# Attention in a vision tower: K for the transport plan by way of DRAM, and a share of each head's result added on VectorE

## What is computed

```python
qn = q / (norm(q) + 1e-8)
C = 1 - einsum('bhnd,bhmd->bhnm', qn, qn);  C = where(eye, 1000, C)
log_K = -C / 0.1
for _ in range(10):                                  # Sinkhorn
    log_u = log_marg - logsumexp(log_K + log_v[..., None, :], axis=-1)
    log_v = log_marg - logsumexp(log_K + log_u[..., :, None], axis=-2)
z = exp(log_u[..., :, None] + log_K + log_v[..., None, :])
z = z / max(z);  z = where(eye, 1, z)
out = softmax(z * hd ** -0.5) @ v
```

## Time and profile before

| what | value |
|---|---|
| median of 3 runs (lowest to highest) | 4995.21 us (4989.33 to 4996.69) |
| the profiled execution's own time, its span | 4997.56 us, 4995.8 us |
| mean granted PE clock | 0.959 |
| attention, 1390 to 3900 us of the span: PE, DVE, ACT busy | 2487.76, 2006.51, 1598.71 of 2510 us |
| DMA over the whole span | 232.97 MB, mean 47 GB/s |

### The profile page before, as it was taken

How to read it: one execution, slowest core, us unless ns; L and a number is a source line. 1 busy time by engine, 2 the same in 40 slices (tenths; PEclk the granted TensorE clock), 3 DMA queues, 4 the chain that set the end, 5 groups by cost and what they waited for, 6 DMA issues and landing times. The chain is left out here.

```text
span 4995.8 us, 192120 instructions
## 1 busy us (share of the span) xinstructions
PE 4573.8 (92%) x84693; PEld 3640.3 (73%) x84710; DVE 3718.4 (74%) x8486; ACT 3097.0 (62%) x4620; POOL 313.9 (6%) x347
## 2 busy tenths in 40 slices
PE   5999999975899999999999999999999879599992
PEld 3777777732688888888888888888888745277771
DVE  8999999944478888887887887777777745355556
ACT  4777777723566666666666666666666326377776
POOL 0000000000000000000000000000000005523331
PEclk9999999987899999999999999999999979699996
DMA  1010000023001111111111122100000024322224
GB/s 64 28 40 28 27 27 27 17 93 81 25 17 32 29 37 29 33 25 23 42 43 36 37 42 52 27 23 16 16 16 15 6 89 158 126 65 72 68 69 162
DMA packets 190201, 232.97 MB, mean 47 GB/s; under 512 B 81024, under 2 KB 159104, under 8 KB 187328
## 3 DMA queue, kind: packets, MB, share of 16 engines
q1 hardware_dynamic: 175872, 189.76, 14.0%
q0 software_dynamic: 13632, 32.66, 1.8%
HBM read 144.09 MB, written 78.25 MB: 45 GB/s over the span
## 5 line engine op out<-in xcount | busy, mean ns | idle before, releaser
L699 PE MATMUL y_ps<-k_sb,x_sb 128*12 128x256 f16 x58368 | 1694.9, 274 | 33.5 <-DVE x_sb L956 24.3
L699 PEld LDWEIGHTS y_ps<-k_sb,x_sb 128*12 128x12 bf16 x58368 | 1427.8, 88 | 218.2 <-issue 37.6
L829 ACT ACTIVATE y_sb<-y_ps 128x256 f32<-128x256 f32 x912 | 348.4, 382 | 856.2 <-PE y_ps L699 856.2
L838 ACT ACTIVATE k_new<-cos,k_bias 128x512 f32<-128x512 f32 x768 | 520.9, 683 | 171.7 <-PE cos L726 171.7
L709 PEld LDWEIGHTS turned_x<-rows_in,y_sb 128*128 128x128 f32 x3648 | 478.3, 191 | 120.2 <-issue 72.7
L987 DVE CUSTOM_DVE_ANT_0 plan<-plan,u_rows,v_last 128x512 f32<-128x512 f32 x768 | 535.2, 744 | 4.1
L709 PE MATMUL turned_x<-rows_in,y_sb 128*128 128x16 f32 x3648 | 527.1, 258 | 9.9 <-ACT y_sb L829 9.2
L257 PE MATMUL acc<-w_hl,feat_h 128*128 128x384 f16 x2688 | 455.3, 327 | 87.5 <-ACT feat_h L242 87.5
L852 ACT ACTIVATE plan<-plan,p_bias,p_scale 128x1024 f32<-128x1024 f32 x384 | 464.1, 1237 | 9.7 <-DVE p_scale L998 9.7
L975 DVE TENSOR_TENSOR plan<-k_sb 128x1024 f32<-128x1024 f16 x384 | 459.3, 1217 | 0.0
L1002 DVE TENSOR_TENSOR k_sb<-k_new,k_sb 128x2048 f16<-128x2048 f32 x192 | 436.2, 2272 | 29.8 <-ACT k_sb L846 29.8
(11 more groups left out here) (261 smaller groups left out, 7223.1 us busy)
## 6 DMA issues: line engine op xcount, KB each, us to landing
x_in_sb<-expert_rows SPq DMA_DIRECT2D x39, 528.0 KB
xt<-in_x_dram SPq DMA_DIRECT2D x16, 1280.0 KB, 5.8
q_left<-q_parts SPq DMA_DIRECT2D x192, 64.0 KB, 3.9
q_right<-q_parts SPq DMA_DIRECT2D x192, 64.0 KB, 3.9
raw<-in_w_dram SPq DMA_DIRECT2D x24, 384.0 KB, 4.3
w<-w_halves SPq DMA_DIRECT2D x16, 576.0 KB, 7.1
w<-expert_results SPq DMA_DIRECT2D x24, 384.0 KB, 6.4
v_parts<-v_sb SPq DMA_DIRECT2D x16, 408.0 KB, 2.4
```

What stands on the lines that cost most here:

```text
L699: last = nc.tensor.matmul(y[a][32 * c:32 * c + XW, :, :], high[:, j, XW * h:XW * (h + 1)], k_sb[s][:, h, :, at:at + P], start=(h == 0 and ...
L829: nc.scalar.activation(y_sb[a][:, :, :], y[a][:, :, :], ACT.Copy).then_inc(rows_read[a], 1)
L838: nc.scalar.activation(k_new[h % 2][:, c, :], cos[:, c % 2, :], ACT.Exp, bias=k_bias[:, 0:1], scale=1.0 / (REG * Q_SCALE ** 2), accum_out= ...
```

## The change

1. `join` goes, on DVE. SP's `store_k` sends each head's float32 `k_new` (1 MB) to `k_all`, a ring of five groups in DRAM, once ACT has written it; `load_k` brings it back into `plan[h]`, which now has four buffers, about one phase before `times_u` wants it. The other new waits: `exponents` for the store from that `k_new` two heads back, `times_u` for the load, `load_k` for the `times_v` that read the buffer last and for the store. `high_parts` no longer waits for `joined`.
2. `turn_v` has only L767's matmul. `normalise` begins with a `scalar_tensor_tensor` that adds (1 - exp(-scale)) times v to the turned result, 128 x 68 values, from PSUM into `lifted`; the reciprocal and the product read `lifted`.
3. The load of v waits for `att_ready` in place of `pv_turned`, since DVE now reads v too. SP clears `project`'s semaphores as it enters `attend`; one constant (`lift`) goes.

```diff
@@ attend, SyncE
+            def store_k(G, h):
+                H = (G + 1) * GH + h
+                after(sp, k_exp, (H + 1) * TB)
+                sp.dma_start(k_all[(G + 1) % RING, h, :, :], k_new[h % 2][:, :, :].rearrange("p b n -> p (b n)")).then_inc(k_out[h % 2], 16)
+
+            def load_k(F, h):
+                after(sp, pv_ready, (F - 1) * GH + h + 1)
+                after(sp, k_out[h % 2], 16 * ((F * GH + h) // 2 + 1))
+                sp.dma_start(plan[h][:, :, :].rearrange("p b n -> p (b n)"), k_all[F % RING, h, :, :]).then_inc(k_in[h], 16)
...
                 if old:
-                    after(sp, pv_turned, (G - 3) * GH)
+                    after(sp, att_ready, (G - 3) * GH)
                     load_v(t - 1 if s == 0 else t, (s + 2) % 3)
+                if build:
+                    store_k(G, 0)
+                if fin:
+                    load_k(G - 2, 3)
                 if tail:
                     after(sp, att_ready, (G - 2) * GH)
                     store(t - 1, s)
-
+                for h in range(1, GH):
+                    if build:
+                        store_k(G, h)
+                    if old:
+                        load_k(G - 1, h - 1)
@@ TensorE
                 after(pe, pv_read, H + 1)
-                nc.tensor.matmul(trp, lift[:, :], v_sb[s][:, :, h, :], start=True, stop=False)
-                nc.tensor.matmul(trp_flat, pv_sb[:, :], to_chunks, start=False, stop=True).then_inc(pv_turned, 1)
+                nc.tensor.matmul(trp_flat, pv_sb[:, :], to_chunks, start=True, stop=True).then_inc(pv_turned, 1)
@@ ScalarE
                     if c == 0:
                         after(act, k_built, H - 1)
+                        after(act, k_out[h % 2], 16 * (H // 2))
...
-                if fin:
-                    after(act, joined, (G - 2) * GH + h + 1)
@@ VectorE
                 if chunks[0] == 0:
-                    after(dve, joined, H + 1)
+                    after(dve, k_in[h], 16 * (F + 1))
                     after(dve, u_rows_ready, H + 1)
...
                 after(dve, pv_turned, H + 1)
-                nc.vector.reciprocal(den[:, :, :], trp[:, :, HD:HD + 1]).then_inc(den_ready, 1)
-                after(dve, den_ready, H + 1)
+                nc.vector.scalar_tensor_tensor(lifted[:, :, :], v_sb[s][:, :, h, :], float(1.0 - np.exp(-ATT_SCALE)), trp,
+                                               ALU.mult, ALU.add).then_inc(den_ready, 1)
+                after(dve, den_ready, 2 * H + 1)
+                nc.vector.reciprocal(den[:, :, :], lifted[:, :, HD:HD + 1]).then_inc(den_ready, 1)
+                after(dve, den_ready, 2 * H + 2)
...
-                nc.vector.tensor_tensor(att_sb[s][:, :, h, :], trp[:, :, 0:HD], den[:, :, :].to_broadcast([P, TB, HD]),
+                nc.vector.tensor_tensor(att_sb[s][:, :, h, :], lifted[:, :, 0:HD], den[:, :, :].to_broadcast([P, TB, HD]),
...
                         if fin:
-                            join(G - 2, new, a, 0)
-                            join(G - 2, new, a, 1)
                             times_u(G - 2, new, a, (0, 1))
```

More of the change, by code:

```diff
@@ L479, in _ @@
             images(dve, nothing, split, read_low)
+    return counters
 GH = 4
@@ L492 @@
 LARGEST_FROM, MAX_PHASE, SPLIT_FROM = 3, 18, 20
+RING = 5
 K_SHIFT = float(15 * np.log(2))
@@ L501, in after, with attend @@
         eng.wait_ge(counter, START + count)
-def attend(nc, q_parts, v_parts, ident, pick_rows, att, w, w_halves, unscale):
+def attend(nc, q_parts, v_parts, k_all, ident, pick_rows, att, w, w_halves, unscale, over):
     with ExitStack() as ctx:
@@ L538, in attend @@
         k_new = two("k_new", [P, TB, TOKENS], F32)
-        plan = two("plan", [P, TB, TOKENS], F32)
+        plan = [sb(f"plan{h}", [P, TB, TOKENS], F32) for h in range(GH)]
         y_sb = two("y_sb3", [P, 2, P], F32)
@@ L571, in attend @@
         cos_ready, k_exp, k_high, k_built = sem("cos_ready"), sem("k_exp"), sem("k_high"), sem("k_built")
-        joined, u_rows_ready, plan_ready, head_max_ready = (
-            sem("joined"), sem("u_rows_ready"), sem("plan_ready"), sem("head_max_ready"))
+        u_rows_ready, plan_ready, head_max_ready = sem("u_rows_ready"), sem("plan_ready"), sem("head_max_ready")
+        k_out, k_in = [sem(f"k_out{a}") for a in range(2)], [sem(f"k_in{h}") for h in range(GH)]
         max_rows_ready, all_max_ready, scale_ready, p_ready = (
@@ L582, in attend @@
         block = ctx.enter_context(nc.Block())
[L583 removed]
+        CONSTS, ZEROS = 6, 7
         def phases(eng, phase):
@@ L670, in phase @@
                     store(t - 1, s)
+                for h in range(1, GH):
[3 more added lines that the diff above has]
+                        load_k(G - 1, h - 1)
+            for counter in over:
+                sp.sem_clear(counter)
             sp.wait_ge(zeroed, START + ZEROS)
@@ L759, in times_v @@
                         last = nc.tensor.matmul(pv[32 * c:32 * c + HD + 1, 0:P], v_sb[s][:, j, h, :],
-                                                plan[h % 2][:, j, c * P:(c + 1) * P], start=(j == 0), stop=(j == TB - 1))
+                                                plan[h][:, j, c * P:(c + 1) * P], start=(j == 0), stop=(j == TB - 1))
                 last.then_inc(pv_ready, 1)
@@ L850, in weights @@
                     after(act, scale_ready, F * GH + h + 1)
-                part = plan[h % 2][:, 2 * half:2 * half + 2, :]
+                part = plan[h][:, 2 * half:2 * half + 2, :]
                 nc.scalar.activation(part, part, ACT.Exp, bias=p_bias[:, 0:1], scale=p_scale[h % 2][:, 0:1]).then_inc(p_ready, 1)
@@ L895, in phase @@
                         exponents(G, new, a, (2, 3))
-                        high_parts(G, new, a, fin)
+                        high_parts(G, new, a)
                     if c == 2 and build:
@@ L907, in phase @@
                         if build:
-                            high_parts(G, new, b, fin)
+                            high_parts(G, new, b)
                         if fin:
@@ L968, in old_x @@
                     split(tr[1], s, x_steps[1], (G - 1) * (OLD - 1) + i, x_new[1])
[L970 to L978, removed]
             def times_u(F, s, h, chunks):
@@ L986, in times_u @@
                 for c in chunks:
-                    last = nc.vector.tensor_tensor_reduce(plan[h % 2][:, c, :], plan[h % 2][:, c, :], u_rows[:, :],
+                    last = nc.vector.tensor_tensor_reduce(plan[h][:, c, :], plan[h][:, c, :], u_rows[:, :],
                                                           v_last[s][:, c, h:h + 1], 0.0, ALU.mult, ALU.max, row_max[:, c:c + 1])
@@ L1070, in phase @@
                         times_u(G - 2, new, a, (2, 3))
-                        join(G - 2, new, b, 0)
                     if c == 2:
@@ L1074, in phase @@
                             low_parts(G, new, a)
-                        if fin:
-                            join(G - 2, new, b, 1)
                     if c == 3:
@@ L1973, in tower @@
         clear(nc, embed(nc, x, freqs, w_tok, h))
-        project(nc, h, wqv, ident, q_parts, v_parts)
+        over = project(nc, h, wqv, ident, q_parts, v_parts)
         unscale = ctx.enter_context(nc.sbuf_tensor("unscale4", [P, 2], F32))
-        attend(nc, q_parts, v_parts, ident, pick_rows, att, mix_w, halves, unscale)
+        attend(nc, q_parts, v_parts, k_all, ident, pick_rows, att, mix_w, halves, unscale, over)
         mix(nc, h, att, ident, mix_w, halves, unscale, soft_rows_out, soft_results_out)
```

7 lines of the change are left out of this document (4 added, 3 removed).

## The result

| kernel | median of 4 runs (lowest to highest) | profiled execution, its span |
|---|---|---|
| before | 4992.27 us (4984.15 to 4996.69) | 4997.56, 4995.8 us |
| after | 5183.32 us (5171.49 to 5201.46) | 5201.46, 5199.4 us |

The ratio is 1.0389, 95% interval 1.0362 to 1.0415: the change makes the kernel 3.9% slower. The forecast of 5091 us had the direction, but the loss is 191 us where 96 were forecast. The range holds the time, and it was wide: from no change to +216 us.

The account below looks back on a forecast made before the run. The prediction took PE as the bound, busy 2487.76 of 2510 us. From the profiled 4997.6 us, -0.6 for the PE and DVE edits and +96 for traffic gave 5093, or 5091 us for the median; range 4984 to 5212.

Parts of the forecast that it names:

- Removed join: 384 DVE instructions, 467 us: worth nothing in steady phases, -4.7 us in the last phase but one.
- new waits: Waits for K's stores and loads, and for `k_new` to be freed: cost nothing at 3 us a transfer.
- late K: Rival: K returns late or `k_new` is freed late, ACT waits in cycle 2; 5041 us at 1 us a phase, chance 0.05.
- -4.7 - 1.7 + 1.1 = -5.3: Last phases: -4.7 us from the join, -1.7 from L766 removed on PE, +1.1 from DVE's new instruction.
- Removed matmul, added DVE instruction: L766 frees 0.25 us of PE per head, but DVE's added 0.25 us makes L739 0.28 us later in cycle 3.
- The terms of the steady phases: PE and DVE edits: cycle 3 +12.6 us, cycle 8 +6.3, cycle 5 -9.9, cycle 0 -4.3.
- 1.0 us these stalls: In before's 14 phases that split weights, PE stalls 1.0 us each during the DMA burst at the phase's start.
- The new traffic, +96 us: K's transfers fill the DMA engines and stall PE: 2.4 us a phase, 110 us over 46 phases, less today's 14.
- 0.11 us of stall for a microsecond of full queue: Rate taken from before's weight-splitting phases; costs 1.7 us for the 15.5 us burst over each phase boundary.
- at half weight: Two lone store and load pairs of 6 us a phase, counted half because PE has instructions in store: 0.7 us.
- The harmless-traffic rival: K's traffic doesn't disturb PE, as two rules of the Trainium skill suggest: 4995 us, chance 0.22.
- Phases "all alike" of 58 us: Sign that the forecast is right: all phases last about 58 us, where harmless traffic would give 55.7 us.

Follow-up runs that it names:

- e1: The kernel before with only the diagonal's share moved to DVE and `lift` gone, join kept and no ring: 5042.3 us, ratio 1.0033 to before.
- e4: The changed kernel without K's stores and loads or the waits for them, `plan` set once on GpSimd: 5031.39 us, ratio 1.002 to before.
- e2: e1 with `normalise` moved behind `times_u` and `head_max` in cycles 3 and 8: 5004.29 us, ratio 0.9947 to before.
- e11: The kernel before with q's loads issued two at a time over seven cycles instead of at the phase's start: 4975.96 us, ratio 0.9956.
- e5: The changed kernel with K's four stores a phase and no loads: 5009.21 us, ratio 1.002 to before.
- e3: The changed kernel with `turn_v`, `normalise` and `lift` as before, so the ring alone: 5209.3 us, ratio 1.0363 to before.
- e7: The changed kernel with each K store and load cut into four of 256 KB, spread over ten cycles: 5032.85 us, ratio 1.0063 to before.
- e10: The changed kernel with each K store and load cut into four of 256 KB, issued where the whole one was: 5132.65 us, ratio 1.0255 to before.

## Why the prediction was right, and where it was off

- **Removed join, new waits, late K.** Right. ACT and DVE wait for no transfer (L863, L999). With before as with e1, 40.9 and 40.2 us pass from the last `turn_x` to the last `turn_v`; with e4 and after 35.2 and 35.0: -5.8 us, where -4.7 - 1.7 + 1.1 = -5.3 were forecast.
- **Removed matmul, added DVE instruction.** Right in mechanism; small in size, and somewhat too small. The new instruction takes 0.25 us from start to start (I took 0.25), and the distance from the end of the multiply to `max_to_rows` opens as forecast. On DVE and PE at 3404 us:

```profile
3400.52 0.22 DVE L1047 SCALAR_TENSOR_TENSOR lifted<-v_in_sb,pv 128x68 f32<-128x68 f32 x1
3400.77 0.18 DVE L1050 RECIPROCAL den<-lifted 128x4 f32<-128x4 f32 x1
```

```profile
3404.14 0.49 PE L764 MATMUL u_rows<-eye_four,head_max 128*128 128x128 f32 x2 [0.41 <-DVE head_max L1004]
```

  The terms of the steady phases sum to 4.7 us over 45, 0.10 a phase; e1 shows 0.12 in nine quiet phases of ten. In total everything but the transfers comes to 5 us (medians) or 10 us (ratio) in e4, where -0.6 was forecast, and 3 us of that are stalls (11.6 against 8.5): a small miss. e2 shows that PE would have had 0.7 us a phase to gain.
- **Stalls in the kernel before.** "1.0 us these stalls" in each phase that splits weights is shown by e11. With no long stall left, its 14 such phases last (3194.41 - 2407.07) / 14 = 56.24 us, 0.93 less than 57.17, and the quiet ones 55.65 as before.
- **The new traffic, +96 us.** The mechanism was right and the size half of what it had to be. The term that was mis-sized is "0.11 us of stall for a microsecond of full queue", with the short bursts "at half weight"; and a term was missing, the clock. The traffic costs some 185 us. The account below is for the profiled executions, from the first to the last `turn_x`, which are 2632.9 us apart in before and 2840.1 in after, 207.2 more.
  - Long stalls: 105 with 148.6 us of idle time, against 9 with 8.5, are 140 us. A stall holds PE for longer than its idle time says, since the profile ends the matmul ahead of it 0.27 us behind its start, where the next one usually starts after 0.03: 96 x 0.24 = 23 us. Together 163 us, where the forecast has 96. The rate isn't constant: idle time and this addition give 0.18 us for a microsecond with a share of 0.9 or more in after, and 0.06 in e5. I carried one rate from the bursts of rows 9 to longer ones.
  - The clock: it is at its lower level, half of full speed, for 89 us in after and 10 in before, and PE is busy for 83 and 10 of them. Half of the difference, 37 us, is lost. The forecast had nothing for this.
  - 7 us are left, of the size of e4's total. The end of the attention, above, gives 5.8 us back.
- **The harmless-traffic rival** is refuted by after against e4, 3.7% apart, and with it what the prediction drew from two rules. By the Trainium skill, "DMA: Bandwidth & Descriptors", section "Queues, rings and completion order", each DMA engine serves its queues in turn, by packets. From this the prediction concluded that a fetch waits for one packet only; here the instruction queue passed nothing in 11 us of a busy queue and three blocks in nine quiet ones. Whether the rule or the conclusion fails, no run tells. The "mostly hidden" of the Trainium skill ("Runtime: NRT & Kernel Launch", section "Instruction fetch mechanics") holds in quiet phases of e11, 11 times 55.65 us without a stall, and not beside a burst.
- **Phases "all alike" of 58 us.** Wrong: 56.7 to 65.3. The same burst costs 1.5 us in one phase and over 4 in another. I didn't test what decides it; how far PE's fetched instructions reach when a burst begins would do it.

That the stall is a wait for the instruction fetch is shown by where the 487 stalls stand and when they end, and that the K transfers make it by e3, e4 and e7. No run changed the fetch itself, and why one burst lets a block through and another doesn't stays open.

## What to carry to other kernels

Traffic that no engine waits for isn't free where PE runs thousands of short instructions: look for DMA shares near 1 that last over some 5 us beside "issue" idle time, and spread the transfers over the phase, in smaller pieces and away from those that are there already. The sign of it is that PE goes on just behind a block of q8. Spreading took the same bytes from 3.9% to 0.6% here, and gained 0.4% in the kernel before. And work taken from the full engine is worth only as much as the chain that hands over to it allows: the same edit was +0.3% or -0.5% by the place of one `normalise`.

## What was unexpected in the hardware

- PE's stall outlasts the burst. In e10 the store and load end by 3412, and PE stands on until 3413.95; the block that it waits for ends at 3412.37. The stretches:

```profile
3409.00:3412.00 3.00, 2.30 (x85) 1.79 (x76) 2.18 (x1) 1.90 (x4) 0.00 (x0) 1.00 0.71 229
3412.00:3415.00 3.00, 1.05 (x30) 0.80 (x29) 0.00 (x0) 0.00 (x0) 0.00 (x0) 0.99 0.01 3
3415.00:3418.00 3.00, 3.00 (x14) 2.45 (x14) 0.81 (x4) 2.29 (x4) 0.00 (x0) 0.50 0.02 5
```

- Idle time of 2.65 us was followed by the clock of 1.2 GHz there, for 6.8 us; at half speed that loses up to 3.4 us, more than the stall itself. It isn't the length of the stall alone: in after 11 of 17 stalls of over 2 us were followed by the lower clock, one of 2.08 us among them (at 3268 us), and one of 3.77 us (at 2890 us) was not.
- Cutting the transfers in four, at the same places, lowered the cost by 1.3 points, though the rows are then 2 KB instead of 8 KB and the packets more: I had taken small packets for the worse case. With as many full microseconds as after, e10 lets more instruction blocks start in them, 159 in 876 (0.18 a microsecond) against 93 in 883. Whether it is the size of the rows or of the transfers, no run separates.
